# The first norm's sums on ScalarE instead of VectorE, in a Mamba and gated feed-forward block with a re-laid order

## The chip, the cores and the metric

One Trainium2 chip, one core. The metric is the device time of one execution in microseconds, the median of several runs.

## The reference

Input x is 16 sequences of 1024 tokens by 256 channels, float32. Then

```python
xz = einsum('btd,pd->btp', x, W_xproj)            # 64 rank + 16 B + 16 C columns
dt = softplus(einsum('btr,dr->btd', xz[..., :64], W_dt) + b_dt)
dA, dBx = exp(dt[..., None] * A), dt[..., None] * Bm[:, :, None, :] * x[..., None]
h_t = dA_t * h_{t-1} + dBx_t                      # 16 states per channel, over 1024 steps
y   = sum_s h_s * C_s + Dp * x
x1  = layernorm(x + y)                            # the first norm
out = layernorm(x1 + (silu(x1 @ wg.T) * (x1 @ wu.T)) @ wd.T)   # int weights / 127, hidden 768
```

layernorm takes mean and variance over the 256 channels of a token, with eps 1e-5 and no affine part.

## The kernel before, in words

The work is cut into 32 chunks of 512 tokens (T), two to a sequence; a step handles one. In a step, each engine goes through 16 slots, one for each state s. Channels lie on partitions, as two halves q of 128, and tokens along the row. The loop over steps is written out for an even chunk (par 0) and an odd one (par 1, whose scans start from h_carry, the last column of the even chunk).

For each state: ScalarE forms the decay exp(dt * A_s), one instruction for each q, into p_da in PSUM (line 533); POOL forms ub = u * B_s (L406) and VectorE scans (L699): h = decay * h + ub. The K states 3, 7, 11, 15 are the other way round: the decay goes to SBUF (da_k), ScalarE forms ub in transposed form (L547) and TensorE turns it into p_da (L928). Then h is multiplied with C_s, by POOL for the POOL_STATES (L416), by VectorE for the rest (L707, with C_s spread into p_c by TensorE, L937), and TensorE adds h, turned to tokens-first, into p_y (L960), SUM_LAG slots later. So when the 16 states are summed, p_y_tok holds z = x + y with tokens on partitions, four groups k of 128 tokens by 256 channels.

Three chunks are in work at a time. Step c scans chunk c; it prepares dt, u, B and C of chunk c + 1 (x_transposed, x_out, project, rank_out, bc_out, project_dt, softplus_abs, softplus_exp, softplus_log, dt_of, u_of, u_transposed, u_out, bc_turned, bc_cols); it does the first norm and gate/up of chunk c - 1, and down, residual and the second norm of chunk c - 2. Six gate/up tiles (gate_up L984, tanh L568, silu L737, hidden L743) follow each other one slot apart.

The first norm: z_out (L552) copies z out of PSUM; norm_stats(0, z) (L713, bn_stats) and norm_mean(0) (L717, bn_aggr) give mean and variance; norm_inputs (L726, L727) adds eps and negates the mean, for both norms at once; POOL's norm_scalars raises to -0.5 (L423) and multiplies (L426); norm1 (L559) applies it on ScalarE, four instructions; TensorE turns x1 (x1_transposed, L974) into p_m; x1_high (L564) and x1_low (L731) form the two float16 halves from which the gate and up matmuls read.

The order of the work is written out by hand. The table AT gives each job a slot and a zone in it: the slot has zones 0 and 1 on ScalarE and POOL, and 0 to 2 on VectorE and TensorE. VectorE's zone 0 ends with scan(s, 0), zone 1 with scan(s, 1), zone 2 with the times_c of state s - 1. ScalarE's zone q ends with the decay of state s + 1, half q, and in even steps slot s ends with the carry copy of state s (L519). POOL has times_b of state s + 4 in zone 0, times_c of s - 1 in zone 1. TensorE sums in zone 1 the POOL state and in zone 2 the VectorE state whose lag has passed. Each engine executes its list in order; semaphores make it wait. TensorE's transposes of the next x, its projections, x1 and gate/up all share the two banks of p_m. SP issues the loads, the stores and the broadcasts of B and C rows.

Two waits matter for the order of the list:

```python
            def decay(c, s, par, q):
                ...
                    wait(act, s_scan, 2 * units(c, s) - 2 + q - 1)   # p_da[:, q] is free again
            def carry(c, s):
                wait(act, s_scan, 2 * units(c, s))
```

## Time and profile before

| | before |
|---|---|
| median of 3 runs (lowest, highest) | 2022.97 us (2020.72, 2024.86) |
| the profiled execution | 2022.87 us |
| its span in the trace | 2021.1 us |
| VectorE (DVE) busy | 1869.1 us, 92% |
| POOL busy | 1768.4 us, 87% |
| TensorE (PE) busy | 1729.2 us, 86% |
| ScalarE (ACT) busy | 1474.9 us, 73% |
| mean granted TensorE clock | 0.947 of full |
| DMA | 110 GB/s over the span, 33.3% of the 16 engines |

Times in the trace count from the start of the span, in microseconds unless marked ns. Consecutive instructions of one engine overlap a little in it, so the time that one takes in a row of many is the distance of two starts and not its duration. The trace holds one execution; a table by line sums over all of it, a timeline shows a stretch with the idle time of the engine before an instruction and what released it.

### The profile page before, as it was taken

To read this page: it belongs to the slowest core of one execution; us is meant where nothing else is said; L and a number is where in the kernel's file an instruction comes from. 1 tells how busy PE (TensorE), PEld (TensorE's weight loads), DVE (VectorE), ACT (ScalarE), POOL (GpSimd) and SP (SyncE) were. 2 spreads that over 40 slices of the span, in tenths; PEclk is the share of its full clock that TensorE was granted. 3 is DMA by queue.
4 is the path that set the end of the run, shared out by engine and by line. 5 is a ranking of instruction groups with operands and counts; after the bars stand their busy time and mean duration, and the time that the engine had idled before them with its cause. 6 is when DMAs were issued, how large, how long until landed. Compare 5 with 4: busy or idle time off the path is not lost.

```text
span 2021.1 us, 35597 instructions
## 1 busy us (share of the span) xinstructions
PE 1729.2 (86%) x10664; PEld 1339.9 (66%) x10664; DVE 1869.1 (92%) x2317; ACT 1474.9 (73%) x2668; POOL 1768.4 (87%) x811
## 2 busy tenths in 40 slices
PE   5688888888889888889888889888889888889887
PEld 3566676666677666777666776666766666766665
DVE  5899999999999999999999999999999999999993
ACT  6767777777777778777677877777777778776752
POOL 5998889988988988988988899989889989889970
PEclk7899999999999999999999999999999999999989
DMA  7234333233333233333234233234233243232300
GB/s 248 95 98 137 104 119 116 86 123 135 105 117 115 83 126 131 105 105 125 89 126 130 96 110 120 100 126 131 95 110 113 96 136 121 99 115 88 112 12 21
DMA packets 102675, 223.18 MB, mean 110 GB/s; under 512 B 9617, under 2 KB 44018, under 8 KB 102642
## 3 DMA queue, kind: packets, MB, share of 16 engines
q1 hardware_dynamic: 102642, 222.78, 33.3%
q8 instruction: 16, 0.26, 0.1%
q14 instruction: 17, 0.14, 0.0%
HBM read 203.87 MB, written 18.87 MB: 110 GB/s over the span
## 4 chain that ended last, share of the span: by engine, by line
PE 49%; issue 15%; ACT 14%; DVE 13%; POOL 7%; DVEq 1%; ACTq 0%; POOLq 0%; DMA 0%; SPq 0%
PE p_o L997 16%; PE p_y L960 13%; PE p_m L984 6%; POOL h L416 5%; DVE h L707 4%; DVE hid L743 3%; DVE h L699 3%; ACT p_da L533 3%; PE p_m L908 3%; PE p_c L937 3%; PE p_m L900 3%; ACT da_k L533 2%; ACT res_n L576 2%; PE p_da L928 2%; DVE silu_g L737 2%
## 5 line engine op out<-in xcount | busy, mean ns | idle before, releaser
L406 POOL TENSOR_TENSOR ub<-u,b_bc 128x1024 f32<-128x1024 f32 x384 | 906.1, 2375 | 0.1
L416 POOL TENSOR_TENSOR h<-h,c_bc 128x1024 f32<-128x1024 f32 x320 | 757.0, 2378 | 0.0
L533 ACT ACTIVATE p_da<-dt,neg_a 128x512 f32<-128x512 f32 x768 | 524.1, 686 | 231.2 <-DVE h L699 229.2
L960 PE MATMUL p_y<-ident,h 128*128 128x128 f32 x4096 | 566.2, 290 | 36.9 <-POOL h L416 36.7
L960 PEld LDWEIGHTS p_y<-ident,h 128*128 128x128 f32 x4096 | 509.7, 150 | 87.0 <-POOL h L416 52.0
L699 DVE TENSOR_TENSOR_SCAN h<-p_da,h_carry,ub 128x512 f32<-128x512 f32 x384 | 474.5, 1266 | 9.2 <-ACT p_da L533 8.3
L699 DVE TENSOR_TENSOR_SCAN h<-p_da,ub 128x512 f32<-128x512 f32 x384 | 452.4, 1208 | 15.0 <-ACT p_da L533 9.3
L997 PE MATMUL p_o<-wt_down,hid 128*128 128x256 f32 x1536 | 352.3, 379 | 3.0 <-DVE res L750 1.6
L997 PEld LDWEIGHTS p_o<-wt_down,hid 128*128 128x128 f32 x1536 | 284.4, 190 | 52.2 <-issue 14.7
L984 PE MATMUL p_m<-x_t,wt_up 128*128 128x512 f16 x744 | 194.3, 384 | 81.1 <-DVE hid L743 81.1
L707 DVE TENSOR_TENSOR h<-h,p_c 128x1024 f32<-128x1024 f32 x192 | 229.9, 1197 | 25.3 <-PE p_c L937 25.3
L568 ACT ACTIVATE tanh_g<-p_m 128x512 f32<-128x512 f32 x186 | 110.7, 595 | 173.3 <-PE p_m L984 173.0
L547 ACT ACTIVATE ub_t<-u_t,bc_t 128x256 f32<-128x256 f32 x512 | 230.0, 497 | 0.4
L984 PE MATMUL p_m<-x_t,wt_gate 128*128 128x512 f16 x744 | 202.7, 397 | 1.0
L423 POOL TENSOR_TENSOR rstd<-var_eps,neg_half 128x8 f32<-128x8 f32 x31 | 50.8, 1638 | 174.0 <-DVE neg_mean L727 174.0
L984 PEld LDWEIGHTS p_m<-x_t,wt_up 128*128 128x128 f16 x744 | 61.2, 99 | 212.8 <-DVE hid L743 157.2
L533 ACT ACTIVATE da_k<-dt,neg_a 128x512 f32<-128x512 f32 x256 | 179.7, 716 | 0.4
L699 DVE TENSOR_TENSOR_SCAN h<-da_k,p_da 128x512 f32<-128x512 f32 x128 | 155.4, 1215 | 16.0 <-PE p_da L928 11.0
L699 DVE TENSOR_TENSOR_SCAN h<-da_k,h_carry,p_da 128x512 f32<-128x512 f32 x128 | 162.2, 1274 | 5.9 <-PE p_da L928 5.5
L937 PE MATMUL p_c<-ident,bc_t 128*128 128x128 f32 x768 | 119.2, 278 | 55.1 <-DVE h L707 54.8
L737 DVE SCALAR_TENSOR_TENSOR silu_g<-tanh_g,p_m 128x512 f32<-128x512 f32 x186 | 124.6, 670 | 33.4 <-ACT tanh_g L568 33.3
L928 PE MATMUL p_da<-ident,ub_t 128*128 128x128 f32 x1024 | 140.2, 275 | 7.7 <-DVE h L699 7.7
(101 smaller groups left out, 1875.7 us busy)
## 6 DMA issues: line engine op xcount, KB each, us to landing
b_bc<-bc_rows_dram SPq DMA_DIRECT2D x128, 768.0 KB, 4.0
c_bc<-bc_rows_dram SPq DMA_DIRECT2D x320, 256.0 KB, 4.2
x_in<-in_L_attn_x SPq DMA_DIRECT2D x32, 512.0 KB, 3.5
out_x<-res_n SPq DMA_DIRECT2D x32, 512.0 KB, 3.0
bc_rows_dram<-bc_rows SPq DMA_DIRECT2D x32, 64.0 KB, 1.6
hid<-in_L_ffn_w_gate SPq DMA_DIRECT2D x1, 768.0 KB, 4.9
hid<-in_L_ffn_w_up SPq DMA_DIRECT2D x1, 768.0 KB, 6.8
res<-in_L_ffn_w_down SPq DMA_DIRECT2D x1, 384.0 KB, 7.2
```

The source lines that it names most:

```text
L406: nc.gpsimd.tensor_tensor(ub[:, i % UB_SLOTS, :, :], u[:, par, :, :], b_bc[:, i:i + 1, :].broadcast_to([P, DH, T]), ALU.mult).then_inc(s_u ...
L416: nc.gpsimd.tensor_tensor(h[:, s % H_SLOTS, :, :], h[:, s % H_SLOTS, :, :], c_bc[:, i:i + 1, :].broadcast_to([P, DH, T]), ALU.mult).then_i ...
L533: nc.scalar.activation(da, dt[:, par, q, :], ACT.Exp, scale=neg_a[:, q, s:s + 1]).then_inc(s_da, 1)
L547: nc.scalar.activation(ub_t[:, i % K_SLOTS, k, :], u_t[:, k, :], ACT.Identity, scale=bc_t[:, par, k, s:s + 1]).then_inc(s_ubt, 1)
L699: nc.vector.tensor_tensor_scan(h[:, s % H_SLOTS, q, :], da, dbx, initial, ALU.mult, ALU.add).then_inc(s_scan, 1)
L707: nc.vector.tensor_tensor(h[:, s % H_SLOTS, :, :], h[:, s % H_SLOTS, :, :], p_c[:, :, :].broadcast_to([P, DH, T]), ALU.mult).then_inc(s_hc ...
L737: nc.vector.scalar_tensor_tensor(silu_g[:, :], tanh_g[:, :], 1.0, p_m[:, 0, :], ALU.add, ALU.mult).then_inc(s_silu, 1)
L928: ins = nc.tensor.transpose(p_da[:, q, k * P:(k + 1) * P], ub_t[:, i % K_SLOTS, k, q * P:(q + 1) * P], ident[:, :])
L937: ins = nc.tensor.transpose(p_c[:, 0, k * P:(k + 1) * P], bc_t[:, par, k, N + s:N + s + 1].broadcast_to([P, P]), ident[:, :])
L960: ins = nc.tensor.matmul(p_y_tok[:, k, q * P:(q + 1) * P], h[:, s % H_SLOTS, q, k * P:(k + 1) * P], ident[:, :], start=False, stop=(s == S ...
L984: ins = nc.tensor.matmul(p_m[:, a, :], w[:, n % DH, j * P:(j + 1) * P], x1_t[:, n // DH, n % DH, :], start=(n == 0), stop=(n == 2 * DH - 1))
L997: ins = nc.tensor.matmul(p_o[:, k % 2, :], hid[:, j, k * P:(k + 1) * P], wt_down[:, j, :], start=(j == 0), stop=(j == NH - 1))
```

## The change

z_out becomes four ScalarE activations that also write the row sums of z; z_mean forms the negated mean, once plain and once divided by 16; z_variance makes four passes of squares of (z - mean) / 16 over 256 columns, whose sums are the variance. VectorE's statistics of z are gone, its norm_inputs serves the second norm alone, and POOL adds eps to the first norm's variance and waits for both parts. The table AT, the set of POOL states (still ten), the lag of VectorE's states (3 to 2) and K_AHEAD (2 to 3) are new. Two weight buffers are laid into z and x1.

```diff
@@ -17,7 +17,7 @@
 X1_SCALE = 2.0 ** 11
 
 
-POOL_STATES = (0, 1, 2, 3, 4, 7, 8, 9, 10, 11)
+POOL_STATES = (0, 1, 3, 4, 6, 7, 8, 9, 10, 11)
 
 
 UB_AHEAD = 4
@@ -25,7 +25,7 @@
 
 C_LAG = 1
 POOL_LAG = 1
-SUM_LAG = {True: 4, False: 3}
+SUM_LAG = {True: 4, False: 2}
 
 
 
@@ -33,22 +33,22 @@
 TILE_STEP = 6
 AT = {
     "weights": (7, 1),
-    "x_transposed": (2, 1), "x_out": (2, 1), "project": (3, 0), "rank_out": (4, 1), "bc_out": (4, 1),
-    "project_dt": (4, 1), "softplus_abs": (5, 1), "softplus_exp": (6, 0), "softplus_log": (6, 1),
-    "dt_of": (7, 1), "u_of": (7, 1),
-    "u_transposed0": (12, 1), "u_out0": (15, 0), "u_transposed1": (15, 0), "u_out1": (15, 1),
-    "z_out": (4, 0), "stats1": (4, 2), "mean1": (5, 1), "norm_inputs": (7, 0), "scalars": (5, 0), "norm1": (7, 0),
-    "x1_transposed": (7, 2), "x1_high": (8, 0), "x1_low": (9, 0),
-    "gate_up": (9, 1), "tanh": (9, 0), "silu": (10, 0), "hidden": (10, 1),
-    "down0": (0, 1), "down1": (1, 0), "down2": (1, 1), "down3": (1, 2),
-    "down4": (3, 0), "down5": (3, 2), "down6": (4, 0), "down7": (4, 1),
-    "residual0": (2, 2), "residual1": (6, 0), "stats2": (6, 0), "mean2": (6, 1), "norm2": (10, 1),
-    "bc_turned": (7, 1), "bc_cols": (9, 1),
+    "x_transposed": (0, 0), "x_out": (1, 0), "project": (1, 2), "rank_out": (3, 0), "bc_out": (3, 1),
+    "project_dt": (4, 1), "softplus_abs": (5, 0), "softplus_exp": (5, 0), "softplus_log": (6, 1),
+    "dt_of": (7, 2), "u_of": (7, 0),
+    "u_transposed0": (12, 0), "u_out0": (13, 1), "u_transposed1": (15, 0), "u_out1": (15, 1),
+    "z_out": (3, 0), "norm_inputs": (6, 1), "scalars": (5, 1), "norm1": (7, 0),
+    "x1_transposed": (7, 1), "x1_high": (8, 0), "x1_low": (9, 0),
+    "gate_up": (9, 0), "tanh": (9, 0), "silu": (9, 2), "hidden": (10, 0),
+    "down0": (0, 1), "down1": (0, 1), "down2": (0, 2), "down3": (1, 0),
+    "down4": (3, 0), "down5": (3, 0), "down6": (3, 1), "down7": (4, 0),
+    "residual0": (3, 0), "residual1": (5, 1), "stats2": (5, 1), "mean2": (5, 2), "norm2": (14, 0),
+    "z_mean": (3, 1), "z_var": (5, 0), "bc_turned": (5, 0), "bc_cols": (7, 0),
 }
 
 
 K_STATES = (3, 7, 11, 15)
-K_AHEAD = 2
+K_AHEAD = 3
 K_SLOTS = 2
 GROUP = 4
 UB_SLOTS = 6
...
@@ -132,6 +132,8 @@
 
         z = sb("z", [P, TT, D], F32)
         x1 = sb("x1", [P, TT, D], F32)
+        w_xproj_rows = x1[0:R + BC, 0, :]
+        w_dt_rows = z[:, 0, 0:DH * R].rearrange("p (q r) -> p q r", q=DH)
         x1_t = sb("x1_t", [P, 2, DH, T], F16)
         tanh_g = sb("tanh_g", [P, T], F32)
         silu_g = sb("silu_g", [P, T], F32)
@@ -142,8 +144,13 @@
 
         w_rows = [hid[:, 3 * n:3 * n + 3, :].rearrange("p j t -> p (j t)") for n in range(2)]
         w_rows += [buffer[:, :, :].rearrange("p k d -> p (k d)")[:, 0:HID] for buffer in (res, res_n)]
-        stats = sb("stats", [P, 2, TT, 6], F32)
-        mean_var = sb("mean_var", [P, 2, TT, 2], F32)
+        stats = sb("stats", [P, TT, 6], F32)
+        mean_var = sb("mean_var", [P, TT, 2], F32)
+        z_sum = sb("z_sum", [P, TT], F32)
+        z_square = sb("z_square", [P, 2, D], F32)
+        z_var = sb("z_var", [P, TT], F32)
+        neg_mean_part = sb("neg_mean_part", [P, TT], F32)
+        eps = sb("eps", [P, TT], F32)
         var_eps = sb("var_eps", [P, 2, TT], F32)
...
@@ -419,7 +430,11 @@
 
             def norm_scalars(c):
 
-                wait(pool, s_ln_in, 2 * c)
+                pool.wait_ge(s_z_var, TT * c)
+                nc.gpsimd.tensor_tensor(var_eps[:, 0, :], z_var[:, :], eps[:, :],
+                                        ALU.add).then_inc(s_z_eps, 1)
+                wait(pool, s_ln_in, 2 * (c - 1))
+                pool.wait_ge(s_z_eps, c)
                 nc.gpsimd.tensor_tensor(rstd[:, :, :], var_eps[:, :, :], neg_half[:, :, :],
                                         ALU.pow).then_inc(s_rstd, 1)
                 wait(pool, s_rstd, c)
@@ -446,8 +461,14 @@
                         elif core and s - POOL_LAG in POOL_STATES:
                             times_c(c, s - POOL_LAG, par, batch)
 
+            def z_scalars(c):
+                pool.wait_ge(s_z_var, TT * (c + 1))
+                nc.gpsimd.tensor_tensor(var_eps[:, 0, :], z_var[:, :], eps[:, :],
+                                        ALU.add).then_inc(s_z_eps, 1)
+                pool.wait_ge(s_z_eps, c + 1)
+                norm_scalars_of(c + 1, 0)
+
             def norm_scalars_of(call, k):
-                pool.wait_ge(s_ln_in, 2 * call)
                 nc.gpsimd.tensor_tensor(rstd[:, k, :], var_eps[:, k, :], neg_half[:, k, :],
                                         ALU.pow).then_inc(s_rstd, 1)
                 pool.wait_ge(s_rstd, call)
@@ -455,9 +476,11 @@
                                         ALU.mult).then_inc(s_ln, 1)
 
             def tail(c):
-                norm_scalars_of(c + 1, 0)
+                z_scalars(c)
+                pool.wait_ge(s_ln_in, 2 * c)
                 norm_scalars_of(c + 2, 1)
                 pool.wait_ge(s_out_ready, c + 1)
+                pool.wait_ge(s_ln_in, 2 * (c + 1))
                 norm_scalars_of(c + 3, 1)
             over_chunks(pool, step, tail)
...
@@ -549,7 +572,23 @@
 
             def z_out(c):
                 act.wait_ge(s_y, N * (c + 1))
-                nc.scalar.copy(z[:, :, :], p_y_tok).then_inc(s_z, 1)
+                for k in range(TT):
+                    nc.scalar.activation(z[:, k, :], p_y_tok[:, k, :], ACT.Identity,
+                                         accum_out=z_sum[:, k:k + 1]).then_inc(s_z, 1)
+
+            def z_mean(c):
+                act.wait_ge(s_z, TT * (c + 1))
+                nc.scalar.mul(neg_mean_part[:, :], z_sum[:, :], -1.0 / (ROOT_D * D)).then_inc(s_z_mean, 1)
+                nc.scalar.mul(neg_mean[:, 0, :], z_sum[:, :], -1.0 / D).then_inc(s_z_mean, 1)
+
+            def z_variance(c):
+                act.wait_ge(s_z_mean, 2 * (c + 1))
+                for k in range(TT):
+                    if k >= 2:
+                        act.wait_ge(s_z_var, TT * c + (k - 1))
+                    nc.scalar.activation(z_square[:, k % 2, :], z[:, k, :], ACT.Square, scale=1.0 / ROOT_D,
+                                         bias=neg_mean_part[:, k:k + 1],
+                                         accum_out=z_var[:, k:k + 1]).then_inc(s_z_var, 1)
 
             def norm1(c, x1=x1):
                 act.wait_ge(s_ln, c + 1)
@@ -602,6 +641,10 @@
                         due = due_at(s, zone)
                         if prev and due("z_out"):
                             z_out(c - 1)
+                        if prev and due("z_mean"):
+                            z_mean(c - 1)
+                        if prev and due("z_var"):
+                            z_variance(c - 1)
                         if nxt and due("x_out"):
                             x_out(c + 1, 1 - par)
...
@@ -659,7 +704,8 @@
         def _(dve):
             nc.vector.memset(rank_t[R:R + 1, :], 1.0).then_inc(s_ones, 1)
 
-            nc.vector.memset(mean_var[:, 1, :, :], 1.0).then_inc(s_ones, 1)
+            nc.vector.memset(var_eps[:, 1, :], 1.0).then_inc(s_ones, 1)
+            nc.vector.memset(neg_mean[:, 1, :], 0.0).then_inc(s_ones, 1)
 
             nc.vector.memset(bc_rows[:, :], 0.0).then_inc(s_ones, 1)
             dve.wait_ge(s_a_exp, 1)
@@ -708,23 +754,20 @@
                                         p_c[:, :, :].broadcast_to([P, DH, T]),
                                         ALU.mult).then_inc(s_hc_dve, 1)
 
-            def norm_stats(k, src):
+            def norm_stats():
                 for t in range(TT):
-                    nc.vector.bn_stats(stats[:, k, t, :], src[:, t, :]).then_inc(s_stats[k], 1)
-
-            def norm_mean(k):
+                    nc.vector.bn_stats(stats[:, t, :], res[:, t, :]).then_inc(s_stats, 1)
+
+            def norm_mean():
                 for t in range(TT):
-                    ins = nc.vector.bn_aggr(mean_var[:, k, t, :], stats[:, k, t, :])
-                ins.then_inc(s_mean[k], 1)
-
-            def norm_inputs(c, prev, last):
-
-                if prev:
-                    wait(dve, s_mean[0], c)
-                if last:
-                    wait(dve, s_mean[1], c - 1)
-                nc.vector.tensor_scalar_add(var_eps[:, :, :], mean_var[:, :, :, 1], EPS).then_inc(s_ln_in, 1)
-                nc.vector.tensor_scalar_mul(neg_mean[:, :, :], mean_var[:, :, :, 0], -1.0).then_inc(s_ln_in, 1)
+                    ins = nc.vector.bn_aggr(mean_var[:, t, :], stats[:, t, :])
+                ins.then_inc(s_mean, 1)
+
+            def norm_inputs(c, call):
+                dve.wait_ge(s_mean, c + 1)
+                dve.wait_ge(s_ln, call - 1)
+                nc.vector.tensor_scalar_add(var_eps[:, 1, :], mean_var[:, :, 1], EPS).then_inc(s_ln_in, 1)
+                nc.vector.tensor_scalar_mul(neg_mean[:, 1, :], mean_var[:, :, 0], -1.0).then_inc(s_ln_in, 1)
 
             def x1_low(c):
                 dve.wait_ge(s_x1_hi, c + 1)
@@ -764,23 +807,18 @@
                             for a in range(2):
                                 if due(f"residual{a}"):
                                     residual(c - 2, a)
-                        if prev and due("stats1"):
-                            wait(dve, s_z, c)
-                            norm_stats(0, z)
                         if last and due("stats2"):
                             wait(dve, s_res, 2 * (c - 1))
-                            norm_stats(1, res)
+                            norm_stats()
                         if nxt and due("dt_of"):
                             dt_of(c + 1, 1 - par)
-                        if (prev or last) and due("norm_inputs"):
-                            norm_inputs(c, prev, last)
+                        if last and due("norm_inputs"):
+                            norm_inputs(c - 2, c)
                         if prev and due("x1_low"):
                             x1_low(c - 1)
                         if zone == 2:
-                            if prev and s == AT["mean1"][0]:
-                                norm_mean(0)
                             if last and s == AT["mean2"][0]:
-                                norm_mean(1)
+                                norm_mean()
                         for chunk, j in tiles("silu", s, zone, 3, c, prev, last):
                             silu_of(chunk, j)
                         for chunk, j in tiles("hidden", s, zone, 3, c, prev, last):
...
@@ -820,29 +850,24 @@
             def tail(c):
                 if N - 1 in DVE_STATES:
                     times_c(c, N - 1, 1, CHUNKS // 2 - 1)
-                dve.wait_ge(s_z, c + 1)
-                norm_stats(0, z)
-                dve.wait_ge(s_stats[0], TT * (c + 1))
-                norm_mean(0)
-                norm_inputs_of(c + 1, 0, c + 1)
                 residual(c - 1, 0)
                 x1_low(c)
                 residual(c - 1, 1)
                 dve.wait_ge(s_res, 2 * c)
-                norm_stats(1, res)
-                dve.wait_ge(s_stats[1], TT * c)
-                norm_mean(1)
-                norm_inputs_of(c + 2, 1, c)
+                norm_stats()
+                dve.wait_ge(s_stats, TT * c)
...
```

The tails follow suit: ScalarE calls z_mean and z_variance behind z_out, VectorE's first-norm statistics fall away, and TensorE waits for s_z at TT times the count.

## Rows read from the trace of the kernel before

**Rows 1.** The page, its first part: busy time of each engine.

```profile
PE 1729.2 (86%) x10664; PEld 1339.9 (66%) x10664; DVE 1869.1 (92%) x2317; ACT 1474.9 (73%) x2668; POOL 1768.4 (87%) x811
```

**Rows 2.** Windows of the steady part: start:end, length, busy us (and instructions) by engine.

```profile
500.00:1000.00 500.00, 435.97 (x2722) 339.35 (x2723) 475.78 (x587) 372.38 (x675) 453.47 (x206) 0.96 0.34 111
1000.00:1500.00 500.00, 439.04 (x2729) 341.87 (x2728) 477.48 (x591) 377.15 (x686) 454.63 (x207) 0.96 0.34 111
```

**Rows 3.** VectorE's dt of the next chunk: min/median/max ns, first and last start.

```profile
L676 DVE SCALAR_TENSOR_TENSOR dt<-p_m,dt x32: 1195/1198/1226, 19.7 to 1875.3; 128x1024 f32<-128x1024 f32 x32
```

**Rows 4.** Waits: who for whom, us in total, times, longest.

```profile
POOL rstd L423 <- DVE neg_mean L727: 174.0, 31, 6.9
...
DVE silu_g L737 <- ACT tanh_g L568: 33.3, 25, 2.0
...
DVE h L699 <- ACT p_da L533: 17.6, 37, 1.3
```

**Rows 5.** Timeline of VectorE, an even step from state 3 on, then an odd one's start.

```profile
1005.60 2.45 DVE L699 TENSOR_TENSOR_SCAN h<-da_k,p_da 128x512 f32<-128x512 f32 x2 [0.61 <-PE p_da L928]
1007.97 2.31 DVE L699 TENSOR_TENSOR_SCAN h<-p_da,ub 128x512 f32<-128x512 f32 x2
1010.20 1.38 DVE L713 BATCH_NORM_STATS2 stats<-z 128x6 f32<-128x256 f32 x4
1011.50 2.32 DVE L699 TENSOR_TENSOR_SCAN h<-p_da,ub 128x512 f32<-128x512 f32 x2
1013.74 0.35 DVE L717 BATCH_NORM_AGGREGATE mean_var<-stats 128x2 f32<-128x6 f32 x4
1014.01 0.65 DVE L750 SCALAR_TENSOR_TENSOR res<-p_o,x 128x512 f32<-128x512 f32 x1
1014.70 1.40 DVE L713 BATCH_NORM_STATS2 stats<-res 128x6 f32<-128x256 f32 x4
...
1019.52 1.22 DVE L707 TENSOR_TENSOR h<-h,p_c 128x1024 f32<-128x1024 f32 x1 [0.88 <-PE p_c L937]
...
1025.96 2.34 DVE L699 TENSOR_TENSOR_SCAN h<-p_da,ub 128x512 f32<-128x512 f32 x2 [0.38 <-ACT p_da L533]
1033.18 0.69 DVE L737 SCALAR_TENSOR_TENSOR silu_g<-tanh_g,p_m 128x512 f32<-128x512 f32 x1 [1.41 <-ACT tanh_g L568]
...
1069.01 2.43 DVE L699 TENSOR_TENSOR_SCAN h<-p_da,h_carry,ub 128x512 f32<-128x512 f32 x2
```

**Rows 6.** Timeline of ScalarE, the same even step.

```profile
1008.80 1.00 ACT L552 COPY z<-p_y 128x1024 f32<-128x1024 f32 x1
...
1015.44 1.02 ACT L507 ACTIVATE dt<-p_m 128x1024 f32<-128x1024 f32 x1 [0.91 <-PE p_m L908]
...
1023.12 2.07 ACT L559 ACTIVATE x<-z,shift,rstd 128x256 f32<-128x256 f32 x4
1025.10 1.28 ACT L533 ACTIVATE p_da<-dt,neg_a 128x512 f32<-128x512 f32 x2
```

**Rows 7.** Groups of ScalarE by line: busy us, mean ns, idle before.

```profile
L547 ACT ACTIVATE ub_t<-u_t,bc_t 128x256 f32<-128x256 f32 x512 | 230.0, 497 | 0.4
...
L519 ACT COPY h_carry<-h 128x2 f32<-128x2 f32 x256 | 46.1, 180 | 1.2 <-DVE h L699 0.8
L515 ACT ACT_TABLE_LOAD x32 | 41.1, 1283 | 0.6
...
L503 ACT COPY bc_t<-p_o 128x128 f32<-128x128 f32 x32 | 8.5, 267 | 0.0
```

**Rows 8.** Timeline of TensorE behind norm1; then a window (granted clock third from the end).

```profile
1025.25 1.97 PE L974 MATMUL p_m<-ident,x 128*128 128x128 f32 x8 [2.38 <-ACT x L559]
1027.58 3.68 PE L960 MATMUL p_y<-ident,h 128*128 128x128 f32 x16 [0.37 <-POOL h L416]
1031.05 1.46 PE L984 MATMUL p_m<-x_t,wt_gate 128*128 128x512 f16 x4
...
1025.20:1031.20 6.00, 5.58 (x25) 5.13 (x26) 5.62 (x6) 4.44 (x9) 6.00 (x4) 0.50 0.09 15
```

39 lines of the change are left out of this document (20 added, 19 removed).

## The prediction

> **What bounds the kernel now.** I read the page first, then the windows of the steady part, then the waits, then the timelines of VectorE, ScalarE and TensorE over one step (one step is one chunk of 512 tokens).
>
> The page gives VectorE 92% of the span, POOL 87%, TensorE 86%, ScalarE 73% [rows 1]. In the steady part VectorE is busy 475.8 and 477.5 us of two stretches of 500 [rows 2]. The step's length is (1875.3 − 19.7) / 31 = 59.9 us [rows 3], so 1000 us hold 16.7 steps and VectorE idles (24.2 + 22.5) / 16.7 = 2.8 us a step. POOL's only notable wait is the one for the norm's inputs, 174.0 us in 31, 5.6 a step [rows 4]. It is caused by the order: its place is (5, 0) and VectorE's is (7, 0). Nothing shows VectorE waiting for POOL, so that wait costs nothing, and shortening it gains nothing. Work taken from VectorE can gain at most itself plus the 2.8.
>
> But the average hides ScalarE. From the copy of z to the end of the first norm it works without a pause except 0.91 us for TensorE [rows 6], and just behind it VectorE waits 0.38 us for a decay [rows 5]. In this stretch, states 4 to 7, the two engines are even. ScalarE's spare time lies elsewhere, and it can't be fetched: p_da has one half per q, so a decay waits for the scan before it, and in even steps the carry copy ties ScalarE to each state's end. The change puts its new work into this stretch.
>
> **What is removed.** Four bn_stats on z: from 1010.20 to 1011.50, 1.30 us; four bn_aggr: 1013.74 to 1014.01, 0.27 us [rows 5]. That is 1.57 us a step of VectorE. The two small scalar operations stay (half as wide).
>
> **What ScalarE gets.** Starts in a row are 0.08 to 0.1 us closer than durations, so I use pitches.
> - z_out: one copy (1.00 us [rows 6], 0.91 in a row of others) becomes four of 256 columns with a sum each. One 256-column operation with a per-partition factor takes 497 ns and two of them 0.90 us less overlap; with factor and bias 4 take 2.07, pitch 0.5 [rows 6, 7]. Each operand costs about 0.09, so one with neither has a pitch of 0.30: 1.2 us.
> - the squares, with one operand (bias), 4 × 0.40 = 1.6 us.
> - two tiny multiplications like the carry copy (180 ns, pitch under 0.1 [rows 7]) and the wait for the last sum: 0.3 us.
> - the accumulator output, a us for each of the eight. No row shows it. Below it is 0 (a gain is excluded: the same columns pass either way); above, a dependent tiny instruction's whole 0.18 [rows 7], doubled to 0.36 if it also breaks the overlap. I take a = 0.1, the pitch of such an instruction queued behind another.
> Together 1.2 + 1.6 + 0.3 + 0.8 − 0.91 = 3.0 us more a step.
>
> The Trainium skill (ScalarE: Activation LUTs, Rules for kernel authors) says additions and multiplications belong on VectorE; by its figures a 256-column pass costs 0.40 us, 0.49 with one pointer operand. The 497 ns agree. In VectorE: DVE Perf Modes (Two Vector instructions with no wait between them) an operation that also writes its accumulator counts as two instructions, said of VectorE; no row shows whether that holds on ScalarE. If it does, a is nearer its upper end.
>
> **The stretch, new order.** It now runs from the end of scan(2) to the first scan of state 8, one state more than before, because z_out goes from (4, 0) to (3, 0). For an even step:
> - VectorE before: 1007.97 to 1025.96 is 17.99 us, less the idle 0.88 and 0.38 = 16.7 [rows 5]. New: − 1.57 + residual0 0.6 + two scans 2.24 = 18.0 (the times_c are two as before: states 2 and 5 for 5 and 6).
> - ScalarE before: 1008.80 to 1025.10 less 0.91 = 15.4 [rows 6]. New: + 3.0 + one more state's two decays and carry copy 1.3 + the copy of the B and C columns 0.2 (267 ns, moved to (7, 0) [rows 7]) + the decay of state 8 that VectorE waits for, 0.65 = 20.6.
> So VectorE stalls 2.6 us, where it stood 1.3. In odd steps scans are longer (two take 2.43 at 1069.01, 2.32 at 1011.50 [rows 5]; 0.6 over ten), the five carry copies fall away (0.4) and ScalarE starts some 0.4 ahead: the stall is about 1.6. Mean 2.1, against 1.0 before: **+1.1 us**. It shows at scan(6, 0), because the squares (1.6 + 4a), the absolute value and the exponential now all stand at (5, 0), and at scan(7, 1) behind the logarithm's two table loads (1.28 each [rows 7]).
>
> **Behind the stretch.** TensorE turns x1 after norm1. Before, it waited 2.38 us there, and then its granted clock was 0.50 (the 1.2 GHz level) from 1025.2 to 1031.2 [rows 8], against 0.96 in the mean [rows 2]: 16 matmuls of the sums took 3.68 us. Gate then starts at 1031.05, norm1's end + 5.95, and VectorE idles 1.41 us for the tanh [rows 5, 8]. In the new order TensorE reaches x1_transposed at (7, 1) right behind the transposes of state 7, which end with scan(6, 1); from there to norm1's end VectorE does a times_c (1.1), a stall of about 1.0, two scans (2.2) and dt_of (1.1), so TensorE waits some 5 us (sum(3), ahead of it before, now stands behind); and because the lag of VectorE's states is 2, three sums (3, 5, 4) instead of two lie between it and gate. At the low clock that is 1.84 more, of which the rise of the clock gives half back if it comes as late after the wake-up as before: gate 0.8 later. The tanh stall becomes 2.2: **+0.8**. ScalarE's x1_high (its transposes begin only behind dt_of at (7, 2)) ends 0.4 after VectorE wants it: **+0.4**.
>
> **The rest of the order.** silu and hidden of a tile now stand side by side in four of six tiles. A dependent neighbour starts after the end instead of 0.08 before it (1014.70 against 1014.66 [rows 5]): 4 × 0.12 = **+0.5**. The stall at state 3 (0.61 for p_da [rows 5]) should go, since residual0 now covers it: **−0.3** on average. p_c's stall of 0.88 is counted above. norm2 at (14, 0) has the room of a K state; hidden. The products of K states start a state earlier (K_AHEAD 3), two of them inside the stretch as before, so nothing. Projection, x's copy and the bc rows come a state earlier on TensorE, ScalarE and SP; they end before their users ask, and the broadcasts of C still number ten, issued behind POOL products as before. POOL gets one tiny addition and loses most of its 5.6 us wait; no gain, and no cost while it is below VectorE's load. The aliases of weight rows only touch the start: nothing.
>
> **Sum.** −1.57 + 1.1 + 0.8 + 0.4 + 0.5 − 0.3 = +0.9 us a step. Over 30 steps that have both neighbours 28 us. At the end, where nothing overlaps, the norm's chain changes by ScalarE's 3.0 + 0.1 less VectorE's 1.57: +1.5. The profiled execution took 2022.87, equal to the median 2022.97: 2022.9 + 29 = **2052**.
>
> **Bounds.** Least: a = 0 (−0.6), tanh stall unchanged (−0.8), no x1_high stall (−0.4), no neighbour cost (−0.5): −1.4 a step, 1981. Most: a = 0.18 (+0.6), clock low until gate is done (+1.2): +2.7 a step, 2105.
>
> **Rivals.** A change of 0.2% is about what a measurement of this kernel can tell.
> 1. *The saving arrives* (0.27). If ScalarE's new pieces fit (a near 0, or its operations closer than I think) and the new TensorE order keeps its clock, VectorE saves its 1.57 in 31 steps, 49 us: 1974; with half eaten by the stretch 1998. For it: VectorE is 95% busy in the steady part, and three of its idles (0.61, 0.88, 1.41) are TensorE's lateness, which the earlier projection could remove. Against: ScalarE's stretch is already even.
> 2. *A wash* (0.20): a small and only the tanh stall grows; 0 to +0.5 us a step, 2020 to 2038.
> 3. *The forecast* (0.43): the ScalarE stretch binds, 2038 to 2070.
> 4. *Worse* (0.10): a at 0.2 or more and the low clock through gate: 2.0 to 2.7 a step, 2083 to 2105. Square could also need another table than the exponentials; two more loads of 1.28 us in the stretch [rows 7] are 2.6 a step, 2130. The Trainium skill (ScalarE: Activation LUTs, Table sets) holds cheap functions to be in every set, by which that doesn't occur; no row here shows Square.
> POOL as the new bound is out: its busy 454.6 us of 500 [rows 2] is 54.4 a step.
>
> The range reaches from the half-saved case to the milder worse case: 1992 to 2086. Faster 0.30 (rival 1 and a little of the wash), same 0.10 (half the wash), slower 0.60 (the rest).
>
> **What would show it.** Right: VectorE waits for p_da about 2 us a step at scan(6, 0), scan(7, 1) and scan(8, 0) (17.6 us in all before [rows 4]); the tanh wait of silu grows from 33 [rows 4] to some 65 us; ScalarE busy up by 95 to 120 us in all; TensorE's mean granted clock falls below 0.947; POOL's wait for the norm's inputs falls below 60 us. Wrong: VectorE busy down by 50 us with its idle unchanged, or ScalarE idle before its decays in states 5 to 7, or the accumulator outputs not to be seen in the pitches.

## The result, and the profile after

| | before | after |
|---|---|---|
| median (lowest, highest) | 2022.48 us (2020.72, 2024.86) | 2148.61 us (2147.36, 2153.99), 4 runs |
| ratio of after to before, 95% interval | | 1.0626 (1.0614 to 1.0639) |
| the profiled execution, its span | 2022.87, 2021.1 us | 2147.36, 2145.5 us |
| mean granted TensorE clock | 0.947 | 0.928 |

The kernel became 126 us slower, four times the 29 us that were forecast, and 63 us beyond the upper end of the range. The page of after, its busy times and the row of the instruction queue q14 (packets, MB, share of the DMA engines):

```profile
PE 1760.0 (82%) x10664; PEld 1373.0 (64%) x10664; DVE 1834.4 (85%) x2058; ACT 1573.3 (73%) x3212; POOL 1776.8 (83%) x844
...
q14 instruction: 147, 1.20, 0.2%
```

VectorE lost 34.7 us of work [rows 1] and ScalarE got 98.4, so the work went where the change puts it. The loss is idle time. In the waits (who for whom, us in total, times, longest) VectorE's are the ones to read, since it carries the load; for [rows 4]:

```profile
POOL rstd L438 <- DVE neg_mean L770: 122.2, 30, 4.2
ACT ub_t L570 <- issue: 79.8, 13, 6.8
DVE h L745 <- ACT p_da L556: 71.4, 78, 3.4
DVE h L745 <- issue: 60.3, 15, 6.2
...
DVE h L745 <- PE p_da L953: 39.0, 28, 2.4
DVE silu_g L780 <- ACT tanh_g L607: 29.7, 36, 1.7
```

Two rows have no counterpart before: ScalarE and VectorE wait for "issue", that is for nothing that the profile shows, 13 and 15 times, once in two steps. They stand at one place, the start of a turn of the loop over chunk pairs. Three timelines of after (start, us, engine, line, operation; idle before it and its releaser), of VectorE, ScalarE and SP's DMA queue there, and the window of that stretch (busy us by engine, granted clock, share of the DMA engines, GB/s):

```profile
1060.15 2.34 DVE L745 TENSOR_TENSOR_SCAN h<-p_da,ub 128x512 f32<-128x512 f32 x2 [3.74 <-issue]
...
1062.51 0.91 ACT L570 ACTIVATE ub_t<-u_t,bc_t 128x256 f32<-128x256 f32 x2 [6.48 <-issue]
...
1052.01 0.40 SPq L333 DMA_DIRECT2D out_x<-res_n  x1
1052.51 0.44 SPq L349 DMA_DIRECT2D b_bc<-bc_rows_dram  x1
1053.06 2.49 SPq L358 DMA_DIRECT2D c_bc<-bc_rows_dram  x4
...
1050.00:1062.00 12.00, 10.87 (x82) 10.12 (x81) 8.26 (x9) 4.92 (x9) 8.63 (x4) 1.00 0.77 214
```

By the profile both engines have everything that they need, and they don't run. Over the whole execution the instruction queue q14 moves 147 packets instead of 17, 8.2 KB each (1.20 MB / 147). At 64 bytes an instruction (the size follows from the page of the Trainium skill that is cited at the end of this section) 8.2 KB are 128 instructions. The excess of 130 is ten in each of the 13 turns: five for each of the two engines. So the first theory was: in the changed kernel the code of the loop is fetched anew at each turn, for both engines, and the fetch stands in the DMA queues beside the broadcasts of B (768 KB) and C (4 x 256 KB), which are behind the store of the last output, and this waits for the second norm, now at (14, 0).

The second reading is the state-3 wait (`p_da L953`), forecast to go. It was to be seen free of the first only after the fetch had been taken away.

### The profile page after: what moved, and what is told of

It is laid out like the page before. It is cut to its first block, busy times and chain, and to the rows that moved or that the text cites. A ratio compares the mean times of both kernels' runs of the same rounds, so it can differ in the third digit from the quotient of the medians.

```text
span 2145.5 us, 35997 instructions
## 1 busy us (share of the span) xinstructions
PE 1760.0 (82%) x10664; PEld 1373.0 (64%) x10664; DVE 1834.4 (85%) x2058; ACT 1573.3 (73%) x3212; POOL 1776.8 (83%) x844
## 4 chain that ended last, share of the span: by engine, by line
PE 37%; DVE 26%; issue 21%; ACT 10%; POOL 4%; DVEq 1%; ACTq 0%; DMA 0%; POOLq 0%; SPq 0%
DVE h L745 14%; PE p_y L985 11%; PE p_o L1022 7%; PE p_m L1009 6%; DVE silu_g L780 4%; DVE h L753 4%; PE p_m L999 3%; PE p_da L953 2%; PE p_m L925 2%; PE p_c L962 2%; ACT da_k L556 2%; ACT L556 2%; DVE dt L722 2%; POOL ub L417 2%; ACT p_da L556 1%
## 5 line engine op out<-in xcount | busy, mean ns | idle before, releaser
L985 PEld LDWEIGHTS p_y<-ident,h 128*128 128x128 f32 x4096 | 522.1, 152 | 56.5 <-issue 25.0
L1022 PE MATMUL p_o<-wt_down,hid 128*128 128x256 f32 x1536 | 347.6, 380 | 3.0 <-DVE res L793 1.6
L570 ACT ACTIVATE ub_t<-u_t,bc_t 128x256 f32<-128x256 f32 x512 | 229.8, 496 | 80.2 <-issue 79.8
L1009 PE MATMUL p_m<-x_t,wt_up 128*128 128x512 f16 x744 | 204.9, 401 | 0.0
L999 PE MATMUL p_m<-ident,x 128*128 128x128 f32 x248 | 60.2, 424 | 147.7 <-DVE dt L722 145.5
L953 PE MATMUL p_da<-ident,ub_t 128*128 128x128 f32 x1024 | 152.2, 279 | 32.7 <-DVE h L745 32.0
L745 DVE TENSOR_TENSOR_SCAN h<-da_k,p_da 128x512 f32<-128x512 f32 x128 | 150.9, 1208 | 27.7 <-ACT da_k L556 16.1
L556 ACT ACTIVATE da_k<-dt,neg_a 128x512 f32<-128x512 f32 x256 | 173.0, 713 | 0.4
L438 POOL TENSOR_TENSOR rstd<-var_eps,neg_half 128x8 f32<-128x8 f32 x31 | 50.7, 1637 | 122.3 <-DVE neg_mean L770 122.2
L1009 PEld LDWEIGHTS p_m<-x_t,wt_gate 128*128 128x128 f16 x744 | 65.3, 100 | 134.1 <-issue 56.9
```

The costliest lines, as they stand in the source:

```text
L556: nc.scalar.activation(da, dt[:, par, q, :], ACT.Exp, scale=neg_a[:, q, s:s + 1]).then_inc(s_da, 1)
L570: nc.scalar.activation(ub_t[:, i % K_SLOTS, k, :], u_t[:, k, :], ACT.Identity, scale=bc_t[:, par, k, s:s + 1]).then_inc(s_ubt, 1)
L745: nc.vector.tensor_tensor_scan(h[:, s % H_SLOTS, q, :], da, dbx, initial, ALU.mult, ALU.add).then_inc(s_scan, 1)
L953: ins = nc.tensor.transpose(p_da[:, q, k * P:(k + 1) * P], ub_t[:, i % K_SLOTS, k, q * P:(q + 1) * P], ident[:, :])
L985: ins = nc.tensor.matmul(p_y_tok[:, k, q * P:(q + 1) * P], h[:, s % H_SLOTS, q, k * P:(k + 1) * P], ident[:, :], start=False, stop=(s == S ...
L999: ins = nc.tensor.transpose(p_m[:, q, k * P:(k + 1) * P], x1[:, k, q * P:(q + 1) * P], ident[:, :])
```

## Experiments on the turn of the loop

The edits change nothing that is computed: they add waits for a semaphore that has long passed (the compiler puts two of them into one instruction) or take superfluous ones away. Counts of an engine's instructions are those of the compiled program, a matmul and an activation with an accumulator output counted as two.

**e1, fewer instructions in ScalarE's loop body** (325 to 313; those before the loop from 274 to 216):

```diff
             def decay(c, s, par, q):
-                act.wait_ge(s_dt, c + 1)
+                if s == 0 and q == 0:
+                    act.wait_ge(s_dt, c + 1)
```

> The changed kernel with the wait for dt kept only on the first decay of a chunk; the other 31 can never wait, since ScalarE runs in order. No engine gets other work. ScalarE's loop body shrinks from 325 to 313 instructions, the whole program of ScalarE from 909 to 778. Theory F (the two stalls without a releaser at the loop's turn, 6.5 us on ScalarE and 3.7 us on VectorE in 13 turns, are instructions fetched again, and depend on how long ScalarE's code is or where it lies): the 130 additional packets of the instruction queue go, ScalarE's issue stall goes, and the time falls by 13 turns x 6 to 7 us, to 2055 to 2075. Rival W (the stall is a wait for work that the profile doesn't name, such as a transfer or a carry): no change, 2148 within 0.3%, with 147 packets.

2143.42 us, ratio 1.0608 (1.058 to 1.0636). Its page and its waits:

```profile
q14 instruction: 81, 0.66, 0.1%
...
DVE h L746 <- issue: 69.2, 22, 5.9
```

ScalarE's 65 packets and its issue wait are gone. VectorE's stay (69.2 us), and cover what was gained: the time fell by 5 us and not by the 73 or more that were expected. **e2, more in the body before** (two such waits in each slot of ScalarE, body 288 to 320):

```diff
+                        if core and zone == 1:
+                            for pad in range(2):
+                                act.wait_ge(s_neg_a, 1)
```

> The kernel before with two waits more in each of ScalarE's slots, on a semaphore that was passed long ago: 320 instructions in the loop body instead of 288, 900 in all instead of 804, no more work. Theory F, by size: once the body is over some length between 288 and 325, ScalarE fetches at each turn; 147 or so packets in place of 17 and 2022 + 13 x 4 to 7 us = 2075 to 2110. [...]

2023.56 us, 1.0000 (0.999 to 1.0009). 83 packets: the refetch is there, and costs nothing, against the 50 us or more that were expected. At the turn of this kernel the DMA engines are nearly idle (busy 13% from 990 to 996 us and 0% in the 6 us behind), and ScalarE waits for the scan anyway (2.08 us at 996.74). So the refetch alone isn't the cost; what it meets at the turn is.

**e3, after with VectorE's body longer** (316 to 334, the length that it had before):

```diff
+                            if core and s < 9:
+                                for pad in range(2):
+                                    dve.wait_ge(s_a_exp, 1)
```

> The changed kernel with VectorE's loop body padded by 18 waits that are long passed, to the 334 instructions that it has in the kernel before (316 in the changed one). Theory F by size alone: no change of the stalls, 2148 to 2155. If it is instead the place of VectorE's code against some boundary (its body became shorter and still stalls, which size can't explain), VectorE's stall of 3.7 us without a releaser changes or goes and the number of instruction packets falls below 147.

2133.54 us, 1.0549 (1.0531 to 1.0566). Its page and waits:

```profile
q14 instruction: 83, 0.68, 0.1%
...
ACT ub_t L570 <- issue: 75.3, 13, 6.4
DVE h L745 <- issue: 3.0, 3, 1.8
```

A longer body stops VectorE's refetch: its length is not what decides. Before the change it was also 334. The waits also stand in the steps written out ahead of the loop, so they move its start too, from 186 to 204. **e4, before with e1's edit:**

> The kernel before with the same 31 of 32 waits for dt left out (ScalarE's body 288 to 277, in all 804 to 674), as the control for the slim changed kernel. Theory F: nothing to gain, 17 packets, 2015 to 2024. If passed waits cost time in themselves, it is faster by up to 0.5%.

2022.35 us, 0.9997 (0.9987 to 1.0006), 16 packets: the superfluous waits cost nothing to be seen.

**e5, only the start of the loop is moved:** waits ahead of it, 55 more instructions on ScalarE (it then starts at instruction 329 of the engine) and 14 on VectorE (200); the bodies stay.

```diff
+            for pad in range(110):
+                act.wait_ge(s_a_exp, 1)
...
+            for pad in range(28):
+                dve.wait_ge(s_a_exp, 1)
```

> The changed kernel with long-passed waits put ahead of the loops, and nothing changed in the loops: 55 instructions more in ScalarE's prologue (the loop starts at instruction 329 instead of 274) and 14 in VectorE's (200 instead of 186). Theory B (the code is fetched in blocks of 128 instructions, as the 8.2 KB packets say; a loop that touches four blocks is fetched again at each turn, one that touches three is kept; all ten placements seen so far agree with block edges near 190, 318, 446, 574 and 702): both loops now touch three blocks, the packets fall to 17 or 18, both stalls at the turn go, and 2148 becomes 2045 to 2075, the rest being what was forecast for ScalarE's stretch. Rival L (only the length counts): no change, 2148, 147 packets. Rival T (the stalls go but something else is late at the turn): packets 17 and over 2100.

2109.96 us, 1.0436 (1.0419 to 1.0454). Page and waits:

```profile
q14 instruction: 18, 0.15, 0.0%
...
DVE h L747 <- ACT p_da L556: 65.3, 69, 4.7
DVE h L747 <- PE p_da L957: 65.3, 37, 2.4
```

The refetch and both issue waits are gone with not one instruction of the loop changed: **38.6 us** (2148.61 less 2109.96) belong to it in this kernel. That is less than the 60.3 us that VectorE waited for issue, and part of the difference stands in another row: for TensorE at state 3 VectorE waits 39.0 us in after and 65.3 in e5. The rest is 88 us and not the 29 that the expectation had: a miss that the next section takes up.

**e7, before with VectorE's start moved** by 60 instructions (the loop then runs from 256 to 590):

```diff
+            for pad in range(120):
+                dve.wait_ge(s_a_exp, 1)
```

> The kernel before with 60 long-passed waits more ahead of VectorE's loop (it starts at 256 instead of 196, and its 334 instructions then reach 590, over the edge near 574). Theory B: VectorE is fetched again at each turn, some 83 packets, a stall without a releaser of 2 to 3 us in 13 turns (the DMA engines are idle there in this order): 2050 to 2065. If only the length counts: 17 packets and 2020 to 2028.

2023.33 us, 1.0007 (0.9998 to 1.0017): right in the packets, a miss in the time. Page and waits:

```profile
q14 instruction: 82, 0.67, 0.1%
...
DVE h L699 <- issue: 5.3, 17, 0.6
```

The refetch came, at 0.3 us a turn. The issue wait thus runs from 0.3 to 6.1 us a turn (79.8 / 13); e6 below tests whether the DMA load at the turn makes the difference. Where each engine's loop starts and ends, and whether it was fetched again:

```text
kept       DVE 196-530 (before)  200-516 (e5)   204-538 (e3)
           ACT 257-545 (before)  216-529 (e1)  199-476 (e4)  329-654 (e5)
refetched  DVE 186-502 (after)  256-590 (e7)
           ACT 274-599 (after)  289-609 (e2)
```

All eleven fit blocks of 128 instructions with edges near 190, 318, 446, 574 and 702: a loop that touches three blocks is kept, one that touches four is not. This rule was made from before, after and e1 to e4; e5 and e7 were built by it, and both did in packets what it said. That there are five packets a turn and not four isn't explained, and what the blocks are was not looked at in any other way. The Trainium skill says of this (Advanced Engine Details and Errata, ISA Cache) that 32 KB of instructions are held in two lines of 256, and (Runtime: NRT & Kernel Launch, Instruction fetch mechanics) that the cost of going on into the next block is "mostly hidden", but that a taken branch to a target outside these two lines has to wait for a fetch. The runs agree with the total, four blocks of 8 KB, of which one may be the one under way (an estimate from the count of three, not shown), and with the wait at the branch. The packet is half of the page's line, and the wait was nearly hidden in e2 and e7 but not in after.

## Experiments on the order and the sums

**e11, the order alone** (the code of before with the list, the POOL states, SUM_LAG and K_AHEAD of after; stats1 at (4, 1), mean1 at (5, 1)), and **e10, the sums alone** (the code of after, shifted as in e5, with the order of before; z_mean (4, 1), z_var (5, 0)):

```diff
-    "z_out": (4, 0), "stats1": (4, 2), "mean1": (5, 1),
+    "z_out": (3, 0), "stats1": (4, 1), "mean1": (5, 1),
```

> The other half: VectorE's statistics kept (stats1 at (4, 1), mean1 at (5, 1)), with the order, the states, the lag and K_AHEAD of the change. The loops stay at three blocks (starts 257 and 196). The stall at state 3 (2.2 us) stays, ScalarE's stretch gets room (VectorE has 1.57 more, ScalarE 3 less), so its stalls of 2.5 us go; VectorE's statistics cost 1.57: against the changed kernel without its fetches (2110) about 1 us a step less, 2070 to 2090. If the order is not the cause: 2022 within 0.5%.

> Half of the change: the sums on ScalarE as in the change, but the order of the kernel before (z_mean at (4, 1), z_var at (5, 0)), both loops at three blocks. By the forecast's working ScalarE's stretch of 16.3 us becomes 19 us, of which 0.9 fills its wait for TensorE, against VectorE's 16.7 - 1.57 = 15.1: it stalls 3 to 4 us in the place of 1.3, with 1.57 saved; +0.5 to +1.3 us a step, 2037 to 2063. If ScalarE's new work is covered: 1975 to 2000.

e11: 2110.35 us, 1.0434 (1.0416 to 1.0451), 20 us above what was expected. e10: 2034.77 us, 1.0063 (1.0046 to 1.008), just below the expected 2037. **Each by itself, the order costs 88 us and the sums 12**; that makes 100, where both at once (e5) cost 88. In the new order the sums cost nothing: e11 and e5 differ by 0.4 us. Waits of e11, then of e10:

```profile
DVE h L699 <- PE p_da L928: 65.8, 43, 2.4
...
DVE h L699 <- ACT p_da L533: 22.4, 39, 1.6
```

```profile
DVE h L747 <- ACT p_da L556: 102.7, 157, 3.9
DVE h L747 <- ACT da_k L556: 26.8, 30, 0.9
```

The two halves show in different waits, though their times don't add up: TensorE's lateness (p_da of PE, 16.5 us before) comes with the order, ScalarE's (p_da of ACT, 17.6 before [rows 4]) with the sums. In e10 VectorE waits 85.1 + 25.5 us more for decays (102.7 less 17.6, 26.8 less 1.3) and gets back 48.6 (its 1.57 in 31 steps), 31.2 of the tanh wait (33.3 to 2.1) and 22.7 of p_c's (25.3 to 2.6): +8, against 12 measured. From e11 to e5 the wait for p_da of ScalarE grows by 42.9 us (22.4 to 65.3), which takes back most of the 48.6 saved.

Why is TensorE late at state 3? First its timeline in before, from the turn of p_c that runs as VectorE starts the scan ahead (996.45) to the K products that the scan of state 3 wants:

```profile
996.59 0.65 PE L937 MATMUL p_c<-ident,bc_t 128*128 128x128 f32 x4 [1.57 <-DVE h L707]
...
999.25 4.05 PE L997 MATMUL p_o<-wt_down,hid 128*128 128x256 f32 x18
...
1004.01 1.04 PE L893 MATMUL p_m<-ident,x_in 128*128 128x128 f32 x8
1004.88 0.60 PE L928 MATMUL p_da<-ident,ub_t 128*128 128x128 f32 x4
...
1007.92 1.88 PE L900 MATMUL p_m<-x_t,wt_proj 128*96 128x512 f32 x4
```

Then the same stretch in e5, the scan itself, and the window (VectorE's busy time is the third):

```profile
1041.01 0.65 PE L966 MATMUL p_c<-ident,bc_t 128*128 128x128 f32 x4
1041.50 1.04 PE L922 MATMUL p_m<-ident,x_in 128*128 128x128 f32 x8
1042.37 4.05 PE L1026 MATMUL p_o<-wt_down,hid 128*128 128x256 f32 x18
...
1047.13 1.46 PE L1026 MATMUL p_o<-wt_down,hid 128*128 128x256 f32 x6
1048.43 1.88 PE L929 MATMUL p_m<-x_t,wt_proj 128*96 128x512 f32 x4
...
1051.02 1.04 PE L957 MATMUL p_da<-ident,ub_t 128*128 128x128 f32 x8
...
1051.74 2.33 DVE L747 TENSOR_TENSOR_SCAN h<-da_k,p_da 128x512 f32<-128x512 f32 x2 [2.37 <-PE p_da L957]
...
1040.80:1051.80 11.00, 11.00 (x68) 9.12 (x66) 8.63 (x10) 7.27 (x17) 8.27 (x5) 1.00 0.58 182
```

TensorE hasn't a gap in 11 us, at full clock, and VectorE has work for 8.63: it waits the 2.37 that are over. The list is almost the one of before. In both kernels p_c's turn, x_transposed (0.87), 24 down matmuls (3.9 + 1.3 = 5.2) and two states' sums (0.87 each) stand ahead of the products, in another order. What e5 has more is the projection (1.7, from 1048.43 to 1050.14), which came behind the products before (1007.92). Before, TensorE needed 8.7 us (996.59 to the end of the first products at 1005.3) and VectorE 8.5; there was no room for 1.7 us more. The wait grew by as much: from 0.61 to 2.37 us in even steps and from 0.29 to 2.01 in odd ones.

**e12, less work on TensorE:** e5 with only two of every six down matmuls in down0 to down3 (it leaves out part of the down product of half of the tokens):

```diff
-                for j in range(3 * half, 3 * half + 3):
+                for j in ((0, 5)[half],) if k < 2 else range(3 * half, 3 * half + 3):
```

> The changed kernel with the loops moved, and of each of down0 to down3 only 2 of the 6 matmuls (the output is then wrong in half of the tokens; 3.5 us less of TensorE in slots 0 and 1, nothing on ScalarE or VectorE). Theory P (TensorE's load ahead of the transposes of state 3 is what makes scan(3, 0) wait 2.0 to 2.4 us, and z_out with it): that wait falls from 65 us in all to under 15, and the time from 2110 by 40 to 65 us, to 2045 to 2070. If the wait only moves to ScalarE, as it did when the projection was moved: 2090 to 2110.

2035.29 us, 1.0059 (1.0043 to 1.0075). Its waits:

```profile
DVE h L747 <- ACT p_da L556: 66.0, 69, 4.7
DVE h L747 <- PE p_da L957: 5.4, 15, 1.2
```

Of the 88 us 75 go, 10 more than was expected at most. ScalarE's row doesn't move and TensorE's falls by 60; the tanh wait falls too, from 35.1 to 22.5. TensorE's load ahead of state 3 is the cause of the wait there. The 75 us aren't the price of the projection's move alone, since e12 leaves out 3.5 us of TensorE a step and the move brought 1.7. **e9, e5 with the projection put back:**

```diff
-"project": (1, 2), "rank_out": (3, 0),
+"project": (3, 0), "rank_out": (3, 1),
```

> The changed kernel with the loops moved and the projection at (3, 0) as before instead of (1, 2), rank_out one zone later at (3, 1). Theory P (scan(3, 0) waits 2.0 to 2.4 us for TensorE's transposes into p_da, because down0 to down3, the projection and two sums stand ahead of them in slots 0 to 2, 10 us of TensorE against 8 of VectorE): 1.7 us of projection less, the stall at state 3 falls from 2.2 to about 0.5 and the time from 2110 to 2055 to 2070. If ScalarE's stretch takes it back (the absolute value then waits for the projection): 2095 to 2110.

2145.16 us, 1.0603 (1.0586 to 1.0621), 35 slower than e5 where 40 to 55 less were expected. Waits:

```profile
DVE h L747 <- ACT p_da L556: 150.9, 132, 4.7
...
ACT rank_t L513 <- PE p_m L929: 92.7, 32, 3.7
...
DVE h L747 <- PE p_da L957: 15.3, 36, 0.7
```

The TensorE wait does go, 50 us of it, down to 15.3 us, about the 16.5 of before: the early projection is what made TensorE late. It comes back as 86 us on ScalarE: rank_out now waits for the projection at the head of ScalarE's queue, 92.7 us against 4.3 in e5, and the decays of VectorE stand behind it. e9 left rank_out and bc_out at (3, 1), where before had them at (4, 1); with all three back in their old places it was not run, so the price of the early projection in time stays open.

**e6, after with norm2 back at (10, 1)**, unshifted, and **e8, e5 with the same edit:**

```diff
-"norm2": (14, 0),
+"norm2": (10, 1),
```

> The changed kernel with the second norm's last part at (10, 1) as before instead of (14, 0); code length and place untouched. SP's store waits for it, and behind the store on SP stand the broadcasts of B (768 KB) and C (4 x 256 KB) that in the changed kernel fill the DMA engines just at the loop's turn. Theory B with this load: the loops are still fetched again, 147 packets, but with the DMA engines free the fetch takes some 2 to 3 us instead of 6.5: 2148 - 13 x 4 = 2085 to 2110. If the load at the turn is no cause: 2148 within 0.5%.

> The changed kernel with both loops moved to where they touch three blocks, and norm2 back at (10, 1). If the two causes are separate, the stalls at the turn are gone (17 or 18 packets) and what norm2's place costs goes too: the 2085 of the run with norm2 alone less its fetch stalls (28 us on ScalarE, part of it covered), 2055 to 2070. If norm2's place cost only because of the fetch: 2105 to 2112.

e6: 2085.31 us, 1.0314 (1.0297 to 1.0331). e8: 2105.04 us, 1.0404 (1.0386 to 1.0421). e6's page and waits:

```profile
q14 instruction: 147, 1.20, 0.2%
...
ACT ub_t L570 <- issue: 28.2, 13, 2.4
```

As many packets as in after, but 2.2 us a turn on ScalarE in place of 6.1 and almost none on VectorE (4.8 us in all). The store and the broadcasts behind it are now issued from 1007.6 to 1021.3, ahead of the turn at 1027.6, and in the 12 us around it (1021.7 to 1033.7) the DMA engines are 21% busy, with 69 GB/s, instead of 77% with 214: with little traffic beside it the fetch is quick. The time fell as expected. Without the refetch norm2's place is worth only 5 us (e5 to e8), with it 63 (after to e6). So what the shift is worth hangs on the order: with norm2 at (14, 0) it saves 38.6 us (after to e5), with norm2 at (10, 1) it costs 20 (e6 to e8, which refetches nothing). VectorE's waits say where these 20 lie: for TensorE at state 3 it waits 49.9 us in e6 and 65.4 in e8 (in even steps 1.1 to 1.5 us against 2.37), for the tanh 21.7 against 34.6. The granted clock is 0.935 against 0.922. That the pause at the turn lets TensorE get ahead for the next step fits this; it is argued and not shown.

**e13, e11 with silu and hidden apart again** (gate_up (9, 1), silu (10, 0), hidden (10, 1), as before):

> The order of the change without its sums (2110), with gate_up, silu and hidden back at (9, 1), (10, 0) and (10, 1), so that a scan stands between a tile's silu and hidden. The forecast's term of 4 x 0.12 us for the neighbours: 2110 - 31 x 0.5 = 2093 to 2098, less if the tanh stall changes too. If the silu and hidden pairs are no cost: 2106 to 2114.

2099.05 us, 1.0374 (1.0355 to 1.0394): −11 us against e11, one short of the 12 to 17 expected. Two neighbouring rows of VectorE's timeline in after:

```profile
1097.92 0.69 DVE L780 SCALAR_TENSOR_TENSOR silu_g<-tanh_g,p_m 128x512 f32<-128x512 f32 x1 [1.31 <-ACT tanh_g L607]
1098.71 0.69 DVE L786 SCALAR_TENSOR_TENSOR hid<-p_m,silu_g 128x512 f32<-128x512 f32 x1
```

A dependent neighbour starts 0.79 us after the start of the other; in e13 the scan behind a hid of the same size starts 0.58 after it (1094.90 to 1095.48): 0.2 each, 4 in a step, 24 us in 30 steps. e13 got these (and 7.6 of the tanh wait), and TensorE's wait at state 3 rose from 65.8 to 83.9, which fits e12: where TensorE's list sets the pace, work taken from VectorE ahead of it comes back as a wait.

**e14, e10 with z_out (3, 1) and z_mean (4, 0); e15, e14 with the copies rank_out and bc_out on VectorE at (4, 2); e16, e15 with z_out (3, 0) and z_mean (3, 1).** The question was whether the sums pay anywhere.

```diff
-                        if nxt and due("rank_out"):
-                            rank_out(c + 1)
...
+                dve.wait_ge(s_proj_ps, c + 1)
+                nc.vector.tensor_copy(rank_t[0:R, :], p_m[0:R, 0, :]).then_inc(s_rank, 1)
```

> The sums on ScalarE in the order of before (2035), with z_out half a slot earlier, at (3, 1), and z_mean at (4, 0): ScalarE waits some 0.5 us in slot 3 and z is summed 2 us before it is copied, so its stretch can begin 0.5 to 1.0 us earlier. As ScalarE bounds the stretch, 31 x 0.5 to 0.8: 2010 to 2020, faster than both kernels. If the stretch's start is set by the scans and not by ScalarE: 2030 to 2037.

> The kernel of e14 (sums on ScalarE, order of before, z_out at (3, 1); 2024) with the two copies of the next chunk's rank rows and B and C rows out of PSUM moved from ScalarE to VectorE, at (4, 2). Theory S (with the sums on it, ScalarE's stretch from z_out to norm1 sets the pace and VectorE stands idle there): ScalarE's stretch loses 2 x 0.5 us, VectorE's 1.2 us fill its idle time; the p_da and da_k waits fall from 99 us by 25 to 35 and the time to 1990 to 2003, faster than both kernels. If VectorE is the bound again: 2024 + 31 x 1.2 = 2050 to 2061.

> The same with z_out at (3, 0) and z_mean at (3, 1). If TensorE has summed z by then, ScalarE's stretch begins a further 0.3 to 0.5 us earlier: 5 to 15 us below e15. If not, z_out waits for the last sum and the decay of state 4 behind it is late: 5 to 30 us above e15.

e14: 2024.01 us, 1.0002 (0.9993 to 1.0011). e15: 2017.0, 0.9967 (0.9955 to 0.9979). e16: 2014.99, 0.9964 (0.9951 to 0.9976). Waits and a window of e15:

```profile
DVE h L743 <- ACT p_da L556: 34.9, 66, 4.7
...
DVE h L743 <- ACT da_k L556: 12.5, 33, 0.5
...
500.00:1000.00 500.00, 436.00 (x2736) 338.92 (x2737) 478.32 (x543) 384.73 (x797) 455.83 (x215) 0.97 0.33 111
```

z_out one zone earlier gives 11 us (e10 to e14), and giving VectorE two copies back for the statistics that it lost gives 7 more (e14 to e15). All three came out above what was expected of them: 2010 to 2020 for e14, 1990 to 2003 for e15, and 5 to 15 us below e15 for e16, which can't be told from e15. In e15 the waits for decays fell further than expected, from 99.0 to 47.4 us, but those for the tanh and for p_c grew from 5.8 to 19.6 and from 1.0 to 12.5. e15 and e16 beat before by 0.3%, an interval that leaves out 1: VectorE is busy 478 of 500 us again [rows 2], and has about as much work as it had (1861.9 us in all against 1869.1).

## Why the prediction was wrong in its size

The direction and the first cause (ScalarE's stretch) held, the size didn't. Us per step. The measured waits are the difference between the wait rows of e5 and of before, divided by 30; the statistics and the neighbours are taken from pitches in the timelines:

| term | predicted | measured |
|---|---|---|
| statistics gone from VectorE | −1.57 | −1.6 |
| ScalarE stretch (p_da, da_k; less p_c) | +1.1 | +1.65 (74.0 − 24.5 us) |
| tanh after the low clock | +0.8 | +0.06 (35.1 against 33.3) |
| x1_high | +0.4 | +0.3 (13.6 against 5.0) |
| silu and hidden side by side | +0.5 | +0.8 (4 x 0.2) |
| state 3, TensorE's p_da | −0.3 | +1.6 (65.3 against 16.5) |
| sum | +0.9 | +2.8, 84 of e5's 88 us |
| code fetched again at the turn | not foreseen | 1.3, 38.6 us |

**The step that failed** is "The stall at state 3 (0.61 for p_da [rows 5]) should go, since residual0 now covers it", together with the early projection put at nothing ("they end before their users ask"). residual0 covers nothing new: in both kernels it stands just ahead of the first scan of state 3 (1004.33 in before, 1048.71 in e5), and VectorE has the same 8.5 us of work up to there, counted from the scan during which p_c's turn runs (996.45 and 1040.87). It was TensorE's list that changed. The projection moved from (3, 0) to (1, 2), ahead of the K products of state 3, and that is 1.7 us more on an engine that was already the later one there. The wait grew by 1.7 us a step in the timeline (1.6 by the rows), and with the projection behind the products it is 15.3 us in all again (e9). The trace of before had what the sum needed: 8.7 us of TensorE against 8.5 of VectorE up to the products, and the projection's 1.7 behind them. 1.9 of the 2.0 us a step between forecast and e5 are this term. The other terms miss by up to 0.7 each and cancel, which is luck.

**What was not in the trace of before** is the refetch. VectorE waits for issue there for 0.6 us in all, and the 17 packets on q14 look like nothing. Nothing in the prediction speaks of code. The change lengthened ScalarE's body by 37 instructions and shortened VectorE's by 18, and moved both starts; both loops went over an edge by it. Nor could the edges be had from the rows. But that norm2, and with it the store and the broadcasts behind it, moved to the turn was in the diff; it was called hidden.

**The ScalarE stretch** was worked out well for the even step. In after the stalls stand where they were placed, at scan(6, 0), scan(7, 1) and scan(8, 0): 1.39, 0.93 (at 1087.62) and 0.53 us (at 1090.49), 2.85 against 2.6 forecast. The first of them:

```profile
1081.96 1.22 DVE L745 TENSOR_TENSOR_SCAN h<-p_da,ub 128x512 f32<-128x512 f32 x1 [1.39 <-ACT p_da L556]
```

Odd steps came to 2.24 and not 1.6 (1.17, 0.60 and 0.47). The 1.0 that stood against it was right for these steps: 0.88 and 0.38 in the even one [rows 5], 0.38 and 0.41 in the odd one of before (1080.39, 1086.94). So the stretch grew by 1.5 us where 1.1 was forecast. The unknown, a, was right. From the same timeline of ScalarE, and its groups:

```profile
1070.14 0.19 ACT L576 ACTIVATION_READ_ACCUMULATOR z<-p_y 128x1 f32 x1
1070.23 0.37 ACT L576 ACTIVATE z<-p_y 128x256 f32<-128x256 f32 x1
...
L589 ACT ACTIVATION_READ_ACCUMULATOR z_square<-z,neg_mean_part 128x1 f32 x128 | 23.9, 187 | 0.0
```

The sum is a second instruction of 187 to 206 ns, and the next starts 0.09 us after it (1070.14 to 1070.23): a = 0.09 where 0.1 was taken. (In the bounds a = 0 was counted as −0.6; eight times 0.1 is 0.8, which would put the lower bound at 1975.) What the Trainium skill says of VectorE (VectorE: DVE Perf Modes, Two Vector instructions with no wait between them), that an accumulator output makes an operation two, is so on ScalarE too. Four copies took 1.44 us (predicted 1.6), the squares 2.1 (2.0). Square costs no table load: 32 + 32 loads as before. The Trainium skill (ScalarE: Activation LUTs, Table sets) says that cheap functions appear in every set and names relu, copy, identity and abs; Square isn't among those named, and the runs show that it behaves like them.

**The tanh.** TensorE waited 4.95 us ahead of the turn of x1 (some 5 forecast; norm1 ended at 1089.7, and the last to end was VectorE's dt at 1090.0), and the granted clock of the 6 us behind it was 0.56, near 1.2 GHz, as forecast:

```profile
1090.10 1.94 PE L999 MATMUL p_m<-ident,x 128*128 128x128 f32 x8 [4.95 <-DVE dt L722]
...
1090.00:1096.20 6.20, 6.10 (x32) 6.13 (x33) 5.40 (x5) 4.97 (x11) 6.17 (x3) 0.56 0.54 184
```

The price didn't follow: VectorE waited 1.31 us for the tanh against 1.41 before [rows 5]. Gate began 6.6 us behind norm1 and not 5.95, 0.6 later where 0.8 was forecast. But its four matmuls took 1.03 us at a granted clock of 1.00 (1096.2 to 1097.2) and not 1.46 at 0.65 (1031.05 to 1032.3), and the 0.31 us that VectorE waits for x1_high stand ahead of silu and hide as much. Two forecast stalls in a row on one engine were added where the first hides part of the second.

Of the signs named: ScalarE busy +98 (95 to 120) and a clock below 0.947 (0.928) came; the stall at states 6 to 8 came; the tanh wait did not grow (29.7, not 65), and POOL's wait for the norm fell to 122.2 and not below 60, since POOL's place (5, 1) still stands a slot ahead of VectorE's (6, 1).

**The rivals.** "The saving arrives" and "a wash" fell with e10: even by themselves, in the old order, the sums cost 12 us, though in e14 a move by one zone makes it a wash. The first of them had the earlier projection on its side, as what could remove TensorE's lateness; at state 3 it did the opposite. "Worse" had the right sign and wrong reasons: a stayed small, the low clock did not last until the gate. That order alone would be the loss wasn't among them.

## What to carry to other kernels

When an order is laid out anew, add up each engine's queue between two fixed points (here, the K products of one state and the next) from the pitches of the rows, for the engines that are "86% busy" too; an engine with 14% to spare over the step can lack 2 us in three slots. Test the parts of a compound change each by itself: here one part cost 88 us, the other 12, and one zone earlier nothing; and expect that they don't add up. If a wait for "issue" shows once a loop turn, look at the packets of the instruction queue first and shift the loop's start by a few dozen instructions: it is a one-line test. It was worth 39 us here, but with the second norm in its old place the same shift cost 20, so it has to be measured each time.

## What the runs showed of the hardware

- Whether a loop's code is fetched again each turn depends on where it lies against blocks of 128 instructions, and not on its length alone: the loop of 316 instructions from 186 on was refetched (5 packets of 8.2 KB a turn), the same from 200 on was kept. Eleven placements fit edges near 190, 318, 446, 574 and 702; what the blocks are was not looked at further.
- A refetch held VectorE for 0.3 us a turn in e7 and ScalarE for nothing to be seen in e2, 2.2 us in e6 and 6.1 in after. In the 12 us around the turn the DMA engines were 21% busy (69 GB/s) in e6 and 77% (214 GB/s) in after. That it competes with the kernel's own transfers is the reading of this pair.
- The accumulator output of a ScalarE activation takes 0.09 us in a row of them (an instruction of 187 to 206 ns), and the next activation still starts before the end of the one ahead (1070.59 against 1070.60).
